# Shared expert of a transformer layer: gate and up from two fp16 parts instead of fp32

## What is computed

```
x = x + attention(layernorm(x))                  # causal, 16 heads, out projection
n = layernorm(x)                                 # the "second norm"
logits = n @ gate_w.T                            # 8 experts, top 2 of the softmax, renormalised
shared = (silu(n @ shared_gate.T) * (n @ shared_up.T)) @ shared_down.T
routed = sum over the 2 chosen e of w_e * (silu(n @ gate_e.T) * (n @ up_e.T)) @ down_e.T
out = x + shared + routed
```

## Time and profile before

| | |
|---|---|
| median of 3 runs | 918.85 us (917.88 to 920.42) |
| the profiled execution | 918.86 us |
| its span, first to last instruction | 917.1 us |
| mean granted TensorE clock | 0.974 |
| shared expert, first to last gate and up | 759.2 to 804.9 us |

### The profile page before, as it was taken

How to read it: one execution, slowest core, us unless ns; L and a number is a source line. 1 busy time by engine, 2 the same in 40 slices (tenths; PEclk the granted TensorE clock), 3 DMA queues, 4 the chain that set the end, 5 groups by cost and what they waited for, 6 DMA issues and landing times.

```text
span 917.1 us, 25699 instructions
## 1 busy us (share of the span) xinstructions
PE 853.2 (93%) x10266; PEld 577.4 (63%) x10266; DVE 695.6 (76%) x1771; ACT 684.9 (75%) x842; POOL 710.7 (77%) x448
## 2 busy tenths in 40 slices
PE   4788999999999999999999999999999787969997
PEld 2345666666666666666666666666666563538886
DVE  7798797888879797989797979787976455445444
ACT  4366888988898889898989898988889782124442
POOL 1466889999999899889989898988889877254442
PEclk9799999999999999999999999999999999779998
DMA  6121232323242424233301020202020001112214
GB/s 181 24 52 65 56 67 65 68 55 68 64 74 50 79 55 86 64 69 73 62 17 42 16 48 1 58 2 48 2 48 3 2 2 44 40 39 69 62 44 145
DMA packets 60149, 48.33 MB, mean 53 GB/s; under 512 B 8688, under 2 KB 57714, under 8 KB 59904
## 3 DMA queue, kind: packets, MB, share of 16 engines
q1 hardware_dynamic: 57760, 42.48, 20.7%
q0 software_dynamic: 2272, 4.22, 1.3%
HBM read 13.93 MB, written 16.29 MB: 33 GB/s over the span
## 4 chain that ended last, share of the span: by engine, by line
PE 60%; DVE 25%; issue 5%; POOL 4%; ACT 3%; DMA 2%; SPq 1%; POOLq 0%; DVEq 0%; ACTq 0%
DVE row_max L1028 10%; PE st L1308 7%; PE st L1309 7%; PE bg L1233 7%; PE pv L1340 5%; PE pv L1342 4%; PE pv L1344 4%; POOL p_parts L585 4%; DVE junk L1024 3%; PE bg L1483 3%; PE bg L1223 3%; PE bg L1200 2%; PE bg L1198 2%; PE bg L1199 2%; DVE att_parts L1050 2%
## 5 line engine op out<-in xcount | busy, mean ns | idle before, releaser
L585 POOL TENSOR_TENSOR p_parts<-prob,p_parts 128x1024 f16<-128x1024 f32 x320 | 612.4, 1935 | 93.5 <-ACT p_parts L720 91.6
L719 ACT ACTIVATE prob<-st,p_bias 128x1024 f32<-128x1024 f32 x320 | 331.1, 1035 | 101.9 <-PE st L1309 72.3
L720 ACT ACTIVATE p_parts<-st,p_bias 128x1024 f16<-128x1024 f32 x320 | 330.8, 1034 | 0.0
L1028 DVE TENSOR_REDUCE row_max<-bg 128x1 f32<-128x512 f32 x384 | 250.6, 685 | 9.4 <-PE bg L1233 8.2
L1340 PE MATMUL pv<-v_parts,p_parts 128*128 128x65 f16 x2176 | 232.7, 193 | 3.2 <-POOL p_parts L585 2.6
L1342 PE MATMUL pv<-v_parts,p_parts 128*128 128x64 f16 x2176 | 233.0, 195 | 0.0
L1344 PE MATMUL pv<-v_parts,p_parts 128*128 128x65 f16 x2176 | 231.9, 192 | 0.0
L1308 PE MATMUL st<-qk_parts 128*128 128x512 f16 (+3 forms) x640 | 221.7, 349 | 7.4 <-ACT p_parts L720 4.6
L1309 PE MATMUL st<-qk_parts 66*128 66x512 f16 (+3 forms) x640 | 220.6, 351 | 0.0
L1340 PEld LDWEIGHTS pv<-v_parts,p_parts 128*128 128x128 f16 x2176 | 202.3, 96 | 28.4 <-DVE attn L1080 9.0
L1233 PE MATMUL bg<-qk_parts 128*128 128x512 f16 (+3 forms) x640 | 210.7, 353 | 9.8 <-DVE row_max L1028 2.1
(11 more groups left out here) (230 smaller groups left out, 1048.3 us busy)
## 6 DMA issues: line engine op xcount, KB each, us to landing
qk_parts<-qk_parts SPq DMA_DIRECT2D x192, 64.0 KB, 2.0
row_dram<-fill SPq DMA_DIRECT2D x8, 1290.0 KB, 10.6
qk_parts<-qk_parts SPq DMA_DIRECT2D x16, 256.0 KB, 3.0
stage_raw<-ffn_w SPq DMA_DIRECT2D x16, 176.0 KB, 2.6
v_parts<-row_dram SPq DMA_DIRECT2D x39, 64.5 KB
qk_parts<-y_dram SPq DMA_DIRECT2D x8, 256.0 KB, 4.7
w_raw<-qkv_w SPq DMA_DIRECT2D x8, 192.0 KB, 2.3
down_w<-ffn_w SPq DMA_DIRECT2D x1, 1536.0 KB, 8.1
```

The costliest lines, as they stand in the source:

```text
L585: nc.gpsimd.tensor_tensor(o, a, b, ALU.subtract).then_inc(p_lo_ready, 1)
L719: nc.scalar.activation(o32, src, ACT.Exp, bias=p_bias[:], scale=D ** -0.5)
L720: nc.scalar.activation(o16, src, ACT.Exp, bias=p_bias[:], scale=D ** -0.5).then_inc(exp_done, 1)
L1028: nc.vector.tensor_reduce(row_max[:, t, c:c + 1], bank, AX_X, ALU.max).then_inc(bg_drained, 1)
```

## The change

The shared expert's gate and up outputs are made by `mm3` from fp16 parts. The weights are split once, in head 11 behind group 9: ScalarE copies 128x768 into `shared_hi`, POOL subtracts into `shared_lo`. The normed tokens are split by block: ScalarE copies `xn` into `xn_hi`, VectorE subtracts into `xn_lo` (both buffers held the first norm's parts and are free by then). For blocks 0 and 1 the copies lie in head 15 behind groups 10 and 14, the subtractions in VectorE's slots 13 and 17. For blocks 2 and 3 the copies follow the copies of L686, and the subtractions stand behind base_sum(0) and behind hidden(5). The first step of a block waits for the subtraction. Down and logits stay in fp32.

```diff
+SHARED_SPLIT = (11, 9)
+TURNED_SLOTS = {10: 0, 14: 1}
+SECOND_LOW_SLOTS = {13: 0, 17: 1}
@@ POOL
+            def split_shared():
+                pool.wait_ge(shared_hi_ready, 1)
+                nc.gpsimd.tensor_tensor(shared_lo[:], shared_w[:, 0:2 * FC * P], shared_hi[:], ALU.subtract
+                                        ).then_inc(shared_lo_ready, 1)
...
                     p_low(h, n)
+                    if (h, n) == SHARED_SPLIT:
+                        split_shared()
@@ ScalarE
+            def split_shared():
+                act.wait_ge(shared_landed, 16)
+                nc.scalar.copy(shared_hi[:], shared_w[:, 0:2 * FC * P]).then_inc(shared_hi_ready, 1)
+
             def turned_xn_copy(b):
-                act.wait_ge(bg_drained, NUMBER["rows_t", b])
-                act.wait_ge(bg_ready, drained(("rows_t", b)))
-                nc.scalar.copy(xn[:, blk(b)], bg[:, NUMBER["rows_t", b] % BGRING, :]).then_inc(bg_drained, 1)
+                if b >= 2:
+                    act.wait_ge(bg_drained, NUMBER["rows_t", b])
+                    act.wait_ge(bg_ready, drained(("rows_t", b)))
+                    nc.scalar.copy(xn[:, blk(b)], bg[:, NUMBER["rows_t", b] % BGRING, :]).then_inc(bg_drained, 1)
+                act.wait_ge(bg_drained, drained(("rows_t", b)))
+                nc.scalar.copy(xn_hi[:, blk(b)], xn[:, blk(b)]).then_inc(second_hi_ready, 1)
...
                     exps(h, n)
+                    if (h, n) == SHARED_SPLIT:
+                        split_shared()
+                    if h == H - 1 and n in TURNED_SLOTS:
+                        turned_xn_copy(TURNED_SLOTS[n])
@@ VectorE
+            def second_low(b):
+                dve.wait_ge(second_hi_ready, b + 1)
+                nc.vector.tensor_tensor(xn_lo[:, blk(b)], xn[:, blk(b)], xn_hi[:, blk(b)], ALU.subtract
+                                        ).then_inc(second_lo_ready, 1)
...
+                    if h == H - 1 and n in SECOND_LOW_SLOTS:
+                        second_low(SECOND_LOW_SLOTS[n])
...
             base_sum(0)
+            second_low(2)
             early_tiles()
             hidden(5)
+            second_low(3)
             table(0, EARLY)
@@ TensorE, gate_up_shared(q)
                 if c == 0:
-                    pe.wait_ge(bg_drained, drained(("rows_t", b)))
-                nc.tensor.matmul(st[:, q % 2, 0, :], shared_w[:, g], xn[:, blk(b)], start=True, stop=True)
-                nc.tensor.matmul(st[:, q % 2, 1, :], shared_w[:, u], xn[:, blk(b)], start=True, stop=True
-                                 ).then_inc(gu_ready, 1)
+                    pe.wait_ge(second_lo_ready, b + 1)
+                x_hi, x_lo = xn_hi[:, blk(b)], xn_lo[:, blk(b)]
+                mm3(st[:, q % 2, 0, :], shared_hi[:, g], shared_lo[:, g], x_hi, x_lo, True, True)
+                mm3(st[:, q % 2, 1, :], shared_hi[:, u], shared_lo[:, u], x_hi, x_lo, True, True).then_inc(gu_ready, 1)
...
             pe.wait_ge(shared_landed, 16)
+            pe.wait_ge(shared_lo_ready, 1)
```

More of the change, by code:

```diff
@@ L246, in layer_kernel @@
         shared_w = sb("shared_w", [P, 3 * FC * P], F32)
+        shared_hi, shared_lo = sb("shared_hi", [P, 2 * FC * P], F16), sb("shared_lo", [P, 2 * FC * P], F16)
         junk = sb("junk", [P, BGRING, BLK], BF16)
@@ L337, in layer_kernel @@
         sqrt_warm = sem("sqrt_warm")
+        shared_hi_ready, shared_lo_ready = sem("shared_hi_ready"), sem("shared_lo_ready")
+        second_hi_ready, second_lo_ready = sem("second_hi_ready"), sem("second_lo_ready")
         xn_hi_ready, xn_lo_ready = sem("xn_hi_ready"), sem("xn_lo_ready")
```

## The result

The changed kernel takes 921.39 us (median of 15 runs, 918.33 to 923.35), the kernel before in the same session 918.35 (15 runs, 914.51 to 922.78): ratio 1.0028, 95% interval 1.0016 to 1.0041. The forecast was 917.2 with a range to 920.0. The time went the other way, to the place that rival 3 names. The profiled execution has a span of 920.9 us against 917.1, so 3.8 us are to be found; that is more than the 3.04 between the medians, since the profiled execution (922.64) lies 1.25 above its median. Executions of one kernel differ in how long the half rate lasts: of the changed kernel's 15, the three with a mean granted clock of 0.970 take 922.5 to 923.4 us, the five with 0.974 take 918.3 to 921.7.

What follows compares the result with a forecast made beforehand. Bound: TensorE's releases held behind POOL's 16-scatter batches, so batch 1's start and TensorE work done before its hold, with TensorE-bound tiles behind. From 918.86 us, -0.8 - 1.2 + 0.3 = -1.7 gave 917.2, range 913.8 to 920.0.

Steps and rivals of the forecast that it cites:

- rival 3: TensorE's gap between 770 and 782 grows over 7 us, half clock lasts longer: 921.7 us, chance 0.10.
- with TensorE 2 us ahead, step 4 and maybe more is released before the hold: Steps 0 to 5, before batch 0's hold: about 2 us saved there gets step 4's result to its reader in time.
- the term for the start of batch 1: Second batch of 16 scatters on POOL starts earlier: -0.8 us, between ends of -0.3 and -1.8.
- Work done before the second hold: Steps 8 to 11 and first tile: tile 0 is past its release before batch 1's hold, -1.2 us.
- Head 15: Added copies on ScalarE and subtractions on VectorE mostly fit idle time: +0.3 us, bounds 0 and 1.3.
- Head 11: Weight split, copy 0.86 us on ScalarE and subtraction 1.6 to 1.85 on POOL, hidden by slack: 0.
- Rival 2: Head 15: VectorE's subtractions wait for POOL's running instruction, 1.3 us instead of 0.3: 918.2 us, chance 0.10.

Runs made afterwards that it cites:

- mm_only: Changed kernel without the second norm's copies and subtractions, its fp16 matmuls reading the first norm's parts: 921.41 us, kernel before 918.45.
- padded: Changed kernel with a fourth fp16 product per gate and up output: 921.15 us, kernel before 917.69; repeated 922.76, kernel before 918.05.
- fp16_early: Changed kernel with fp16 gate and up in steps 0 to 5 only, fp32 in 6 to 11: 917.13 us, kernel before 917.69.
- after_again: Changed kernel, unchanged, rerun in a session without holds: 895.17 us, kernel before 897.92, ratio 0.9965.
- aux_only: Changed kernel with gate and up put back to fp32 matmuls, all added work kept: 919.36 us, kernel before 918.45; without holds 898.16, kernel before 897.92.

## Why the prediction was wrong

*The step that failed: "with TensorE 2 us ahead, step 4 and maybe more is released before the hold", and with it the term for the start of batch 1.* I took the hold's start as fixed, 2 to 3 us behind the 9th scatter's issue, from two catches in one trace. It isn't. In the changed kernel step 3's work ends at 766.9, ahead of that issue (768.77), and is delivered 3 us late, and step 4's, done at 769.1, not until the hold's end. In the traces of holding sessions, with no break in the scatters, Silu 4 comes 16.5, 18.4 or 22.7 to 22.9 us behind the first scatter. Nor is all that is caught kept to the end: step 2's down in the kernel before, done at 772.3, reached VectorE at 778.97. The end did hold: 781.2 and 821.07 are 3.5 and 3.7 us behind the issue of the 16th scatters (777.71 and 817.38), and 12.4 and 12.6 us behind that of the 9th. So the term "-0.8" came out as +2.2. Its inner parts were near: from the router's matmuls to ranks(1) it is 9.33 us (786.76 to 796.09) instead of 10.29, 1.0 less where I had 1.1, and the copies and splits there sat in idle time. They only began 3.1 us late.

*"Work done before the second hold"*, -1.2, turned into +1.6. Tile 0's work, done 1.7 us behind the 9th scatter (808.43), was kept to the end of the hold; in the profile of before, done 2.1 us behind it, it got out at 814.58, in mid-hold. So being done sooner behind the 9th scatter did not let it out. Steps 8 to 11 were also worth less than the 1.6 us that I had: from ranks(1) to the end of tile 0's gate and up it is 14.0 us instead of 14.5.

*Rival 3* named the point, TensorE's gap over 7 us; it was 9.32, the half-rate stretch grew from 13.7 to 17.1 us, and the time that it gave, 921.7, is 0.3 off the median. That the sum came out so near is in part luck. Its price was composed otherwise: the router waited for the release (3.1 us), and from there to ranks(1) no time was lost against the profile of before, where the clock was at half too, until 792.1. No row gives the 4.5 us of it; the stretches at half rate grew by 3.4 each. How long they last differs between executions, so the single profile of before wasn't a firm ground for it either. I gave it 0.10 because "the same downs still stand between the waits". The downs did stand there, but the first of them, step 3's, waits for base_sum(0) on VectorE (L1150), and that stands in VectorE's order behind step 4's product (L1144). VectorE of the changed kernel, and then of the kernel before:

```profile
781.83 0.69 DVE L1144 TENSOR_TENSOR prob<-prob,st 128x512 f32<-128x512 f32 x1 [8.71 <-ACT prob L769]
782.43 0.68 DVE L1150 TENSOR_TENSOR res<-res,pv 128x512 f32<-128x512 f32 x1
```

```profile
776.08 0.69 DVE L1112 TENSOR_TENSOR prob<-prob,st 128x512 f32<-128x512 f32 x1 [3.56 <-issue]
778.97 0.69 DVE L1118 TENSOR_TENSOR res<-res,pv 128x512 f32<-128x512 f32 x1 [2.20 <-remote]
```

and TensorE of the kernel before, the row that answers to 783.22 above:

```profile
779.76 3.75 PE L1398 MATMUL pv<-prob,shared_w 128*128 128x512 f32 x4 [4.87 <-issue]
```

With Silu 4 caught until 781.20, base_sum(0) ends at 783.1 and TensorE goes on at 783.22; before it ended at 779.7 and TensorE went on at 779.76. I had read the 4.87 us of TensorE's gap as one wait behind POOL, and not looked for who ends it. The gap and the 3.1 us of the router both end with the release of step 4's gate and up: in mm_only, padded and fp16_early, where it is as late, the router's matmuls start as late too, 28.3 to 28.4 us behind the first scatter instead of 24.6. Whether step 2's down was also held until then the trace can't show, since VectorE was waiting for Silu 4.

*Head 15:* +0.3 predicted, about +1 seen. Batch 0 starts at 758.32, ahead of the 759.00 of before, but only because head 15 began 1.9 us earlier in that execution (first exp at 707.99, before 709.87). From there to the first scatter it is 50.33 us instead of 49.13, and in the free session 51.30 instead of 50.01. Over all traces it is 49.0 to 50.2 us in the five without the added work in this head and 49.0 to 51.4 in the fifteen with it, 49.6 and 50.5 on average. Behind the exp of group 10, where the additions begin, it is 24.5 us in four of the five (26.0 in one) and 25.6 to 26.0 in all fifteen. *Head 11:* the copy takes 0.85 us and the subtraction 1.66 (predicted 0.86, and 1.6 to 1.85), hidden: from its first exp to that of head 12 it is 44.73 us, before 44.75. The matmuls are 1.29 us a step, as predicted.

*Rival 2* has its lock in the trace, and its price of 1.3 us is near what head 15 took. VectorE and POOL in head 15 (the first and second split; POOL's two subtractions in one row):

```profile
740.60 2.39 DVE L1100 TENSOR_TENSOR xn_lo<-xn,xn_hi 128x512 f16<-128x512 f32 x1
742.91 0.17 DVE L1108 RECIPROCAL rden<-pv 128x4 f32<-128x4 f32 x1
...
751.16 0.68 DVE L1100 TENSOR_TENSOR xn_lo<-xn,xn_hi 128x512 f16<-128x512 f32 x1
```

```profile
738.23 4.21 POOL L591 TENSOR_TENSOR p_parts<-prob,p_parts 128x1024 f16<-128x1024 f32 x2 [0.44 <-ACT p_parts L740]
747.00 4.22 POOL L591 TENSOR_TENSOR p_parts<-prob,p_parts 128x1024 f16<-128x1024 f32 x2 [0.40 <-ACT p_parts L740]
```

The first split, beside POOL's second subtraction, takes 2.39 us, 1.7 more, and ends 0.5 us behind POOL's 742.44; the second split starts just as POOL's ends (751.22) and takes 0.68. That is as the rule in the Trainium skill, SBUF — State Buffer, section "SBUF: two separate sides", has it. It is no accident of one trace: after_again has 2.39 and 0.68 us too. What stood behind it came later by it: the reciprocal starts 2.92 us behind the copy into `xn` (739.99) instead of 1.79, in either session. How much of that reaches the end isn't separated; all the added work together costs 0.9 us in a holding session (aux_only) and 0.2 in a free one.

*What stays open.* That the loss sits in the holds is shown from two sides: in a session without them the same kernel is 2.75 us faster than the kernel before, and with a break in GpSimd's scatters alone, which puts either kernel 3 to 6 us below the kernel before, the two are level. Some 5.8 us of the change's worth, +3.0 to -2.75, hang on them. Why the fp16 steps have step 4's release caught later, with four products too, isn't settled, nor is what holds the releases, nor what lets tile 0 out in two traces of the eight without a break. One observation, no more: the listing of DMA issues, whose last figure is the median from issue to landing, has none for the scatters in the changed kernel's holding trace (nor in that of the kernel before), and in the free one 2.5 and 2.4 us.

```profile
row_dram<-attn,place_u POOLq DMA_INDIRECT x16
row_dram<-v_parts,place_u POOLq DMA_INDIRECT x16
```

```profile
row_dram<-attn,place_u POOLq DMA_INDIRECT x16, 2.5
row_dram<-v_parts,place_u POOLq DMA_INDIRECT x16, 2.4
```

Whether a session holds isn't the program's doing: the kernel before took 917.7 to 918.5 us (medians) in four sessions and 897.5 and 897.9 in two, and never both in one. One chip number stands for a session of either kind, so the number doesn't tell them apart.

## What to carry to other kernels

When a reader starts many us behind its producer's end and the row names no program dependency, that wait is the bound: work taken off the producer can then be worth nothing until the wait is broken, and its sign is open. Here the same change was worth +3.0 us with the wait, about 0 with it broken in batch 0 and -2.75 without it. Don't take the onset of such a wait from one trace; price each item that is near its edge as caught and as free, with what stands queued behind it. Take more than one trace of the same kernel before reading a difference of 2 us off two profiles: the return of the full clock alone moved batch 1 by that much. Try a break in the long run of DMA issues first, here one wait in each batch of 16, and judge the matmul change again after it and in a session without the wait.

## What the runs showed that I had not expected

- The same kernel has two levels by session, 918 and 897.5 us (2.3%), all of it between 769 and 819 us: step 3's Silu comes 9.9 us behind the first scatter in both traces, tile 1's Silu at 818.89 and 798.99, and from there to the end it is 98.2 us in both.
- With 16 indirect scatters issued without a break (1.28 us each), releases of TensorE's work come up to 12 us late (769.1 to 781.2, 810.1 to 821.07), the last of them 3.3 to 3.8 us behind the last issue. With batch 0 broken after eight for 5.5 us either kernel is 3 to 6 us below the kernel before, and with both batches broken for 2.2 to 2.4 us the changed one is 9.8 us below.
- A VectorE subtraction of 128x512, both inputs in SBUF, took 2.39 us instead of 0.68 beside a GpSimd subtraction of 128x1024.
